# Attention: ACT copies the turned q and k whole out of PSUM, and Pool subtracts their first parts

## The chip, the cores and the metric

The kernel runs on one core of a Trainium2 chip. The metric is the device time of one execution in microseconds (us). The engines of the core are TensorE (PE; its weight loads are shown as PEld), VectorE (DVE), ScalarE (ACT), GpSimd (Pool) and SyncE (SP), which issues transfers.

## The reference

The program is a mixture-of-experts feed-forward layer, then causal attention, then the same feed-forward layer again, on x of 8 x 1024 tokens and 256 channels. The change touches only the attention:

```
q, k, v = (heads(Wq, bq), heads(Wk, bk), heads(Wv, bv))      # 16 heads of 16 dims, y = x W^T + b
q = _apply_rope(q, cos, sin)
k = _apply_rope(k, cos, sin)
att = jnp.einsum('bhqd,bhkd->bhqk', q, k) * (1.0 / np.sqrt(D))
att = jnp.where(causal[None, None], att, NEG_BIG)
att = jax.nn.softmax(att, axis=-1)
y = jnp.einsum('bhqk,bhkd->bhqd', att, v)
```

## The kernel before

The tokens are 64 tiles of 128. A pair of tiles n (32 pairs) is *prepared*: DVE normalises it (L1505), PE transposes it, multiplies with the weights, DVE adds the biases (L1518 for q and k, L1524 for v), Pool rotates q and k (L1402, L1405, L1410, function rope), and PE turns each tile s of the pair back into the bank prep_ps (L1769, transpose_qk). The attention multiplies q and k in bf16, so each 32-bit number is split into three bf16 parts. For tile s this goes round three engines: ACT copies prep_ps to part[0] as bf16 (first_parts, L1665), DVE writes rest = prep_ps - part[0] (leave, L1532), ACT copies rest to part[1] as bf16 (second_parts, L1670), and Pool writes part[2] = rest - part[1] (third_parts, L1414). SP stores the parts to DRAM (L1294) and the v rows (L1297); they are loaded again by group.

A *group* g is four heads of one batch, 32 groups in all. Group g walks through 12 steps t of one half of the queries by one tile of keys. In each step PE makes four scores (L1797, with L1800 for the causal mask) into three banks that take turns, ACT makes the exponentials from them (L1683), and PE multiplies with v (L1810, times_v). For the group after it, PE makes the products for the maxima of the rows (L1786, ring) into three other banks; DVE takes the maxima (L1559 with the mask, L1562 without) and gives the bank back. DVE also splits the maxima into parts (L1576 to L1583), PE turns them (L1779), and Pool issues their transfer (L1426).

The order on each engine is written out by hand. The first five pairs are prepared in a row (the head); then group g finishes pair g+5 (parameter finish) and prepares pair g+6 (prepare). Before the change, in group g: ACT does first_parts(0) after the exponentials of step 1; second_parts(0) and first_parts(1) after those of step 3; second_parts(1) after step 5; and copies the output o (L1675) after step 4. DVE does leave(0) in step 2 and leave(1) in step 4, each after the maxima of its share; in steps 2 and 3 it also measures pair n+1: L1482, L1487, then L1491 and L1492, L1496, L1499 on 128x2 numbers. Pool does the rotation of tile 1 at t = 0 and 1, third_parts at t = 3 and 5, and adds the output bias to x at t = 4 (add_output_bias, L1420); Pool does not wait for the steps, only for its inputs, and takes its list in order. In the head, Pool's list for a pair is: the rotations of both tiles, L1420, then third_parts(0) and (1); DVE does leave(0) and leave(1) after the biases; ACT does first_parts(0), second_parts(0), first_parts(1), second_parts(1), and then the next pair's copy L1660.

PE's transposes of tile 1 and the next pair's transposes (L1730) use the same bank prep_ps, so they wait until leave has read it (rest_ready).

Of the kernel before, what the change touches and what calls it, by code (L numbers as in the profile page):

```python
# [18 lines left out]
ALU = mybir.AluOpType  # L19
# [3 lines left out]
P = 128  # L23
# [1121 lines left out]
def attention_block(nc, sh, dr):  # L1145
# [6 lines left out]
    with ExitStack() as ctx:  # L1152
# [6 lines left out]
        def sem(n):  # L1159
            return ctx.enter_context(nc.semaphore(f"at_{n}"))  # L1160
# [29 lines left out]
        part = [parts[:, a] for a in range(PARTS)]  # L1190
        rest = [sb(f"rest{k}", [P, 2 * CC, P], F32) for k in range(2)]
# [13 lines left out]
        prep_ps = ps("prep_ps", [P, 2 * C])  # L1205
# [17 lines left out]
        rope_step = sem("rope_step")  # L1223
        rot_ready = sem("rot_ready")
        rt_ps_ready = sem("rt_ps_ready")
        part0_ready = sem("part0_ready")
        rest_ready = sem("rest_ready")
        part1_ready = sem("part1_ready")
        part2_ready = sem("part2_ready")
# [147 lines left out]
        def _(pool):  # L1377
# [9 lines left out]
            def rope(n, s, stage):  # L1387
# [20 lines left out]
                if stage == 2:  # L1408
                    pool.wait_ge(rope_step, at + 2)
                    p.tensor_tensor(rot[s][:], by_cos[:], by_sin[:], ALU.add).then_inc(rot_ready, 1)  # L1410

            def third_parts(n, s):
                pool.wait_ge(part1_ready, 2 * n + s + 1)
                p.tensor_tensor(part[2][:, :, s * P:(s + 1) * P], rest[s][:], part[1][:, :, s * P:(s + 1) * P],  # L1414
                                ALU.subtract).then_inc(part2_ready, 1)
# [15 lines left out]
            for n in range(LEAD - 1):  # L1431
                invert_std(n + 1)
                for s in range(2):
                    for stage in range(3):
                        rope(n, s, stage)
                add_output_bias(n)
                for s in range(2):
                    third_parts(n, s)
            invert_std(LEAD)
            for stage in range(3):  # L1440
# [6 lines left out]
            def body(g, k, more, prepare, finish):  # L1447
                n = g + LEAD
                for t in range(NS):
                    if finish:  # L1450
                        if t <= 1:
                            rope(n - 1, 1, t + 1)
                        if t in (3, 5):
                            third_parts(n - 1, t // 4)
                    if prepare and t == 4:
                        add_output_bias(n)
                    if t == 6 and more:
                        move_peaks(g + 1, slot_round(g, k, 1)[0], 0)
                    if prepare:
                        if 5 <= t <= 7 and n + 1 < PAIRS:  # L1460
                            invert_std(n + 1, [t - 5])
                        if 8 <= t <= 10:
                            rope(n, 0, t - 8)
                        if t == 11:
                            rope(n, 1, 0)
                if more:
                    move_peaks(g + 1, slot_round(g, k, 1)[0], 1)
# [4 lines left out]
        def _(dve):  # L1472
# [53 lines left out]
                                           bias[:, 2 * C:3 * C].rearrange("p (g h d) -> p g h d", d=D, h=GH), ALU.add)  # L1526
                last.then_inc(v_ready, 1)

            def leave(n, s):
                dve.wait_ge(part0_ready, 2 * n + s + 1)  # L1530
                dve.wait_ge(part2_ready, 2 * n)
                v.tensor_tensor(rest[s][:], prep_ps[:].rearrange("p (c t) -> p c t", t=P),  # L1532
                                part[0][:, :, s * P:(s + 1) * P], ALU.subtract).then_inc(rest_ready, 1)

            def ring(g, k, r):

                after_last = isinstance(g, int) and g == GROUPS
# [66 lines left out]

            for n in range(LEAD - 1):
                head(n)
                for s in range(2):
                    leave(n, s)
            head(LEAD - 1)
            for r in range(NR):  # L1610
                if RING[r] == SECOND:
# [7 lines left out]
            def body(g, k, more, prepare, finish):  # L1619
                n = g + LEAD  # L1620
                for t in range(NS):
                    if t == 8 and g >= NG and g % NG == 2:
                        dve.wait_ge(sums_loaded, 16 * (g // NG))
                        v.reciprocal(sums[:], sums[:]).then_inc(sums_inverted, 1)
                    for c in range(SHARES):
                        ahead = ring_group(g, t)
                        if ahead is not None:
                            for r in share(t, c):
                                if has_place(ahead, r):
                                    ring(ahead, (k + (2 if t == NS - 1 else 1)) % SLOTS, r)  # L1630
                        if finish:
                            if (t, c) == (2, 0):
                                leave(n - 1, 0)
                            if (t, c) == (4, 1):
                                leave(n - 1, 1)
                        if prepare:
                            if (t, c) == (1, 2):
                                normalize(n)
                            stage = SHARES * (t - 2) + c - 1
                            if 0 <= stage < 6 and n + 1 < PAIRS:  # L1640
                                measure(n + 1, [stage])
                            if (t, c) == (5, 3):
                                xt_low(n)
                            if (t, c) == (7, 1):
                                add_bias_qk(n, 0)
                            if (t, c) == (8, 3):
                                add_bias_v(n)
                            if (t, c) == (11, 1):
                                add_bias_qk(n, 1)
# [4 lines left out]
        def _(act):  # L1654
# [7 lines left out]
            def first_parts(n, s):  # L1662
                act.wait_ge(rt_ps_ready, 2 * n + s + 1)
                act.wait_ge(stored, 16 * PAIR_STORES * n)
                a.copy(part[0][:, :, s * P:(s + 1) * P], prep_ps[:].rearrange("p (c t) -> p c t", t=P)  # L1665
                       ).then_inc(part0_ready, 1)

            def second_parts(n, s):
                act.wait_ge(rest_ready, 2 * n + s + 1)
# [52 lines left out]
        def _(pe):  # L1722
# [38 lines left out]
            def transpose_qk(n, s, half):  # L1761
                if half == 0:
                    pe.wait_ge(rot_ready, 2 * n + s + 1)
                    if s == 0:
                        pe.wait_ge(qk_ready, 2 * n + 2)
                    else:
                        pe.wait_ge(rest_ready, 2 * n + 1)
                for c in range(CC * half, CC * (half + 1)):
                    last = te.transpose(prep_ps[:, c * P:(c + 1) * P], rot[s][:, c * P:(c + 1) * P], sh.ident[:])  # L1769
                if half == 1:  # L1770
                    last.then_inc(rt_ps_ready, 1)
# [44 lines left out]
            pe.wait_ge(ones_ready, 1)  # L1816

            def head(n):
                pe.wait_ge(rest_ready, 2 * n)
                transpose_x(n)  # L1820
                for i in range(3):
                    product_qk(n, 0, i)
                for s in range(2):
                    product_v(n, s)
                for i in range(3):
                    product_qk(n, 1, i)
# [23 lines left out]
            def body(g, k, more, prepare, finish):  # L1850
                n = g + LEAD
                for t in range(NS):
# [11 lines left out]
                    def piece(c):  # L1864
# [5 lines left out]
                        if not prepare:  # L1870
                            return
                        if (t, c) == (5, 0):
                            pe.wait_ge(rest_ready, 2 * n)
                            transpose_x(n)
                        for i in range(3):
                            if (t, c) == (6, i + 1):
# [121 lines left out]
```

## Time and profile before

| | |
|---|---|
| time, median of 3 runs (lowest, highest) | 2623.69 us (2612.97, 2627.59) |
| the profiled execution, time and span | 2642.3 us, 2640.5 us |
| PE busy | 2226.4 us (84%) |
| DVE busy | 1690.9 us (64%) |
| ACT busy | 1249.4 us (47%) |
| Pool busy | 942.5 us (36%) |
| mean granted clock of PE | 0.922 |

Busy time is the time in which an engine works on an instruction; waits are not in it. The attention takes about 600 to 2000 us of the span. Matmuls are pipelined, so PE's busy time is more than the time in which it takes in columns. In the rows, "idle before" is the idle time of the engine in front of an instruction, and "<-" names what ended it.

### The profile page before, as it was taken

How to read it: one execution, taken by the hardware profiler on the slowest of the kernel's cores; microseconds unless marked ns; L12 is line 12 of the kernel's file. 1: busy time of each engine (PE TensorE's matmuls, PEld its weight loads, DVE VectorE, ACT ScalarE, POOL GpSimd, SP SyncE). 2: the span in 40 equal slices, each digit the busy share in tenths (PEclk: the TensorE clock that was granted, in tenths of full speed). 3: DMA queues.
4: the chain of work that ended last, by engine and by line, in shares of the span. 5: the costliest groups of instructions: out<-in, count | busy, mean ns of one | idle time of the engine just before them, and what ended most of it. 6: DMA issues, size and time to landing. Idle time of an engine off the chain costs nothing. (4 is left out here: it accounts for less than half of the span.)

```text
span 2640.5 us, 43228 instructions
## 1 busy us (share of the span) xinstructions
PE 2226.4 (84%) x14740; PEld 1457.2 (55%) x14740; DVE 1690.9 (64%) x5140; ACT 1249.4 (47%) x2506; POOL 942.5 (36%) x1344
## 2 busy tenths in 40 slices
PE   5739999945599999999999999998994773899997
PEld 5729999943334444443444444443332673799997
DVE  7326556533378778788887877887772662465563
ACT  1224444421046656666666665666673432344443
POOL 3534344316523333333333333332000465244442
PEclk9999999975579999999999999999997875999999
DMA  9372322221624453544534435335324423422220
GB/s 347 147 245 69 109 80 72 72 75 40 155 57 100 102 118 81 122 101 99 118 90 114 109 80 114 98 89 118 83 55 125 161 93 126 167 73 97 92 73 22
DMA packets 187148, 283.22 MB, mean 107 GB/s; under 512 B 14616, under 2 KB 149976, under 8 KB 178736
## 3 DMA queue, kind: packets, MB, share of 16 engines
q1 hardware_dynamic: 172592, 247.08, 34.2%
q0 software_dynamic: 14336, 33.38, 3.6%
q8 instruction: 117, 1.92, 0.3%
q14 instruction: 103, 0.84, 0.1%
HBM read 153.99 MB, written 126.88 MB: 106 GB/s over the span
## 5 line engine op out<-in xcount | busy, mean ns | idle before, releaser
L1683 ACT ACTIVATE at_probs<-at_score_ps 128x512 f32<-128x512 f32 (+3 forms) x1536 | 692.5, 497 | 451.3 <-PE at_score_ps L1800 312.0
L1559 DVE CUSTOM_DVE_ANT_0 at_junk<-at_max_ps,at_causal 128x128 f32<-128x128 f32 (+3 forms) x1024 | 485.3, 484 | 124.8 <-PE at_max_ps L1786 123.2
L1786 PE MATMUL at_max_ps<-at_k,at_q 96*128 96x512 bf16 (+3 forms) x1536 | 493.1, 339 | 44.1 <-DVE at_peak L1559 32.0
L1797 PE MATMUL at_score_ps<-at_q,at_k 99*128 99x512 bf16 (+3 forms) x1536 | 498.0, 331 | 9.2 <-DMA at_v<-v_rows 4.2
L1562 DVE TENSOR_REDUCE at_peak<-at_max_ps 128x1 f32<-128x512 f32 x512 | 351.9, 687 | 114.4 <-PE at_max_ps L1786 111.5
L1786 PEld LDWEIGHTS at_max_ps<-at_k,at_q 96*128 96x128 bf16 x1536 | 144.3, 98 | 398.7 <-DVE at_peak L1559 193.6
L1056 DVE TENSOR_TENSOR f_hid_lo<-f_hid,f_hid_hi 128x512 fp32r<-128x512 f32 x256 | 177.4, 693 | 285.2 <-ACT f_hid_hi L1080 274.6
L1810 PE MATMUL at_o_ps<-at_probs,at_v 128*32 128x512 f32 (+3 forms) x3072 | 336.8, 511 | 1.2 <-ACT at_probs L1683 0.7
L1077 ACT ACTIVATE f_hid<-f_hid_ps 128x512 f32<-128x512 f32 x256 | 153.1, 598 | 377.4 <-PE f_hid_ps L1103 374.1
L1118 PE MATMUL f_y_ps<-f_w_hi,f_hid_hi 128*128 128x256 f32 x1024 | 290.7, 284 | 18.5 <-DVE f_hid_lo L1056 18.5
L1118 PE MATMUL f_y_ps<-f_w_hi,f_hid_lo 128*128 128x256 f32 x1024 | 291.1, 284 | 0.0
L1118 PE MATMUL f_y_ps<-f_w_lo,f_hid_hi 128*128 128x256 f32 x1024 | 290.1, 283 | 0.0
L979 POOL TENSOR_SCALAR f_xn<-f_xe 128x256 f32<-128x256 f32 x120 | 164.1, 1374 | 183.1 <-PE f_xt_ps L1091 134.1
L1402 POOL TENSOR_TENSOR at_by_cos<-at_qk,at_cos 128x512 f32<-128x512 f32 x64 | 70.2, 1098 | 436.7 <-DVE at_qk L1518 436.7
L1800 PE MATMUL at_score_ps<-at_hide_bf,ident_bf 128*128 128x128 bf16 x1024 | 225.4, 222 | 0.0
L1797 PEld LDWEIGHTS at_score_ps<-at_q,at_k 99*128 99x128 bf16 x1536 | 150.5, 98 | 123.6 <-ACT at_probs L1683 74.0
L1118 PEld LDWEIGHTS f_y_ps<-f_w_hi,f_hid_hi 128*128 128x128 f32 x1024 | 194.3, 190 | 30.5 <-DVE f_hid_lo L1056 19.4
L1118 PEld LDWEIGHTS f_y_ps<-f_w_lo,f_hid_hi 128*128 128x128 f32 x1024 | 194.0, 189 | 10.4
L1118 PEld LDWEIGHTS f_y_ps<-f_w_hi,f_hid_lo 128*128 128x128 f32 x1024 | 194.0, 189 | 0.0
L1103 PE MATMUL f_hid_ps<-f_xt_hi,f_w_hi 128*128 128x512 f32 x512 | 168.2, 410 | 2.8 <-DVE f_xt_lo L1025 2.8
L1080 ACT CAST f_hid_hi<-f_hid 128x512 fp32r<-128x512 f32 x256 | 159.0, 621 | 8.2
L1103 PE MATMUL f_hid_ps<-f_xt_lo,f_w_hi 128*128 128x512 f32 x512 | 162.3, 398 | 0.0
(178 smaller groups left out, 3647.8 us busy)
## 6 DMA issues: line engine op xcount, KB each, us to landing
f_w_raw<-in_w SPq DMA_DIRECT2D x32, 1024.0 KB, 7.7
qk<-at_parts SPq DMA_DIRECT2D x32, 768.0 KB, 4.2
expert_in<-r_zeros SPq DMA_DIRECT2D x16, 1040.0 KB, 15.9
f_xe<-expert_in SPq DMA_DIRECT2D x32, 520.0 KB, 4.0
v_rows<-at_v_outs SPq DMA_DIRECT2D x32, 512.0 KB, 6.2
at_v<-v_rows SPq DMA_DIRECT2D x32, 512.0 KB, 10.6
o_rows<-at_o_out SPq DMA_DIRECT2D x64, 256.0 KB, 2.0
at_q<-qk SPq DMA_DIRECT2D x32, 384.0 KB, 7.7
```

Of the source, the lines that this page charges most:

```text
L979: last = nc.gpsimd.tensor_scalar(xn[:, t, :], x[:, t, 0:C], x[:, t, MEAN:MEAN + 1], x[:, t, RSTD:RSTD + 1], ALU.subtract, ALU.mult)
L1056: v.tensor_tensor(hid_lo[f % NHID][:], hid[f % NHID][:], hid_hi[f % NHID][:].bitcast(F32), ALU.subtract).then_inc(hid_lo_ready, 1)
L1080: nc.scalar.copy(hid_hi[f % NHID][:], hid[f % NHID][:]).then_inc(hid_hi_ready, 1)
L1103: last = nc.tensor.matmul(hid_ps[f % 2][:], w[ws][:, cc, f * P:(f + 1) * P], x[b % 2][:, cc, :], start=(i == 0), stop=(i == 3 * CC - 1))
L1118: last = nc.tensor.matmul(y_ps[b % 2][t // 2][:, t % 2, :], a[m][:, rows], w[ws][:, f, :], start=(f == 0 and i == 0 and t % 2 == 0), stop= ...
L1559: v.tensor_tensor_reduce(junk[bank(k, r)][:, 0:w], src, causal[:, HALF - w:HALF], 1.0, LEAST, ALU.add, ALU.max, out).then_inc(max_used, 1)
L1562: v.tensor_reduce(out, src, AX.X, ALU.max).then_inc(max_used, 1)
L1683: a.activation(probs[t % 2][:, h, c0:c0 + w], score_ps[(GH * t + h) % BANKS][:, 0:w], ACT.Exp, scale=float(SCALE)).then_inc(exp_done, 1)
L1786: te.matmul(max_ps[bank(u, r)][:, 0:w], q[u][0:ROWS, h, i * P:(i + 1) * P], kk[u][0:ROWS, h, k0:k0 + w], start=True, stop=True).then_inc(m ...
L1797: last = te.matmul(out[:, 0:w], kk[u][:, h, j * P:(j + 1) * P], q[u][:, h, hf * HALF + c0:hf * HALF + c0 + w], start=True, stop=not diagonal)
L1800: last = te.matmul(out[:, 0:P], sh.ident_bf[:], hide_bf[:], start=False, stop=True)
L1810: last = te.matmul(o_ps[h * VW:(h + 1) * VW, c0:c0 + w], vv[u][:, j, h, :], probs[t % 2][:, h, c0:c0 + w], start=(t == FIRST_STEP[hf]), st ...
```

## The change

ACT's first_parts makes a second copy of the bank, whole and in 32 bits, into rest[s], and signals it with a new semaphore, whole_ready; the second copy waits until the third parts of the pair before are made (part2_ready), as leave did. The subtraction rest = rest - part[0] moves from DVE to Pool and now has two SBUF operands. On Pool, leave(0) stands at t = 2 and leave(1) at t = 4 ahead of add_output_bias; in the head both stand after add_output_bias and ahead of the two third_parts. PE's waits for the bank prep_ps are now for whole_ready, so for ACT's second copy. The semaphore part0_ready is gone.

```
+            def leave(n, s):                       # Pool
+                pool.wait_ge(whole_ready, 2 * n + s + 1)
+                p.tensor_tensor(rest[s][:], rest[s][:], part[0][:, :, s * P:(s + 1) * P], ALU.subtract
+                                ).then_inc(rest_ready, 1)
...
                 add_output_bias(n)                  # Pool, head
                 for s in range(2):
+                    leave(n, s)
+                for s in range(2):
                     third_parts(n, s)
...
+                        if t in (2, 4):             # Pool, groups
+                            leave(n - 1, t // 4)
                         if t in (3, 5):
                             third_parts(n - 1, t // 4)
...
-            def leave(n, s):                       # DVE
-                dve.wait_ge(part0_ready, 2 * n + s + 1)
-                dve.wait_ge(part2_ready, 2 * n)
-                v.tensor_tensor(rest[s][:], prep_ps[:].rearrange("p (c t) -> p c t", t=P),
-                                part[0][:, :, s * P:(s + 1) * P], ALU.subtract).then_inc(rest_ready, 1)
...
-                            if (t, c) == (2, 0):
-                                leave(n - 1, 0)
-                            if (t, c) == (4, 1):
-                                leave(n - 1, 1)
...
             def first_parts(n, s):                  # ACT
                 act.wait_ge(rt_ps_ready, 2 * n + s + 1)
                 act.wait_ge(stored, 16 * PAIR_STORES * n)
-                a.copy(part[0][:, :, s * P:(s + 1) * P], prep_ps[:].rearrange("p (c t) -> p c t", t=P)
-                       ).then_inc(part0_ready, 1)
+                turned = prep_ps[:].rearrange("p (c t) -> p c t", t=P)
+                a.copy(part[0][:, :, s * P:(s + 1) * P], turned)
+                act.wait_ge(part2_ready, 2 * n)
+                a.copy(rest[s][:], turned).then_inc(whole_ready, 1)
...
-                        pe.wait_ge(rest_ready, 2 * n + 1)      # PE: transpose_qk; head and step 5 alike
+                        pe.wait_ge(whole_ready, 2 * n + 1)
```

## Rows read from the trace of the kernel before

**Rows 1.** Waits, 900 to 2000 us: total, times, longest in us
```profile
PEld at_max_ps L1786 <- DVE at_peak L1559: 162.5, 249, 1.2
...
PEld at_score_ps L1797 <- ACT at_probs L1683: 64.0, 155, 0.8
```

**Rows 2.** Stretches: length; PE, PEld, DVE, ACT, Pool busy (instructions), PE clock, DMA share, GB/s
```profile
1203.40:1211.80 8.40, 7.23 (x61) 3.16 (x58) 8.33 (x28) 7.42 (x19) 4.32 (x5) 1.00 0.01 2
1212.00:1215.00 3.00, 3.00 (x15) 0.85 (x16) 2.12 (x8) 0.28 (x1) 0.00 (x0) 0.50 0.28 102
1253.00:1256.00 3.00, 2.77 (x23) 1.15 (x23) 3.00 (x11) 1.99 (x8) 0.00 (x0) 1.00 0.23 87
```

**Rows 3.** Timeline of PE, from 1206 us: start, duration, what, idle before
```profile
1211.92 0.61 PE L1786 MATMUL at_max_ps<-at_k,at_q 96*128 96x512 bf16 x1 [0.75 <-DVE at_peak L1559]
```

**Rows 4.** Timeline of DVE, 1203 to 1214 us
```profile
1204.78 1.10 DVE L1505 TENSOR_SCALAR at_xn<-x_sb,at_moments,at_rstd 128x256 f32<-128x256 f32 x2
...
1206.28 0.68 DVE L1532 TENSOR_TENSOR at_rest<-at_prep_ps,at_parts 128x512 f32<-128x512 f32 x1
1206.88 0.67 DVE L1559 CUSTOM_DVE_ANT_0 at_junk<-at_max_ps,at_causal 128x512 f32<-128x512 f32 x1
...
1209.02 1.19 DVE L1491 TENSOR_SCALAR at_half<-at_moments 128x2 f32<-128x2 f32 x1
...
1211.16 0.69 DVE L1559 CUSTOM_DVE_ANT_0 at_junk<-at_max_ps,at_causal 128x512 f32<-128x512 f32 x1
...
1213.35 0.68 DVE L1532 TENSOR_TENSOR at_rest<-at_prep_ps,at_parts 128x512 f32<-128x512 f32 x1
```

**Rows 5.** Three DVE lines, 830 to 1780 us: ns min/median/max, first and last start
```profile
L1491 DVE TENSOR_SCALAR at_half<-at_moments x23: 169/1203/1215, 840.6 to 1741.9; 128x2 f32<-128x2 f32 x23
...
L1496 DVE TENSOR_SCALAR at_bits<-at_bits x23: 156/157/624, 841.3 to 1743.7; 128x2 int32<-128x2 int32 x23
...
L1505 DVE TENSOR_SCALAR at_xn<-x_sb,at_moments,at_rstd x48: 400/535/780, 836.3 to 1778.7; 128x256 f32<-128x256 f32 x48
```

**Rows 6.** Timeline of Pool, 1203 to 1213 us
```profile
1204.14 1.28 POOL L1410 TENSOR_TENSOR at_rot<-at_by_cos,at_by_sin 128x512 f32<-128x512 f32 x1
1207.81 1.16 POOL L1414 TENSOR_TENSOR at_parts<-at_rest,at_parts 128x512 bf16<-128x512 f32 x1 [2.40 <-ACT at_parts L1670]
1208.93 1.26 POOL L1420 TENSOR_TENSOR x_sb<-x_sb,at_bp 128x512 f32<-128x512 f32 x1
```

**Rows 7.** Groups, 900 to 2000 us: busy us, mean ns | idle before, releasers
```profile
L1414 POOL TENSOR_TENSOR at_parts<-at_rest,at_parts 128x512 bf16<-128x512 f32 x46 | 53.2, 1157 | 167.0 <-ACT at_parts L1670 167.0
...
L1675 ACT COPY at_o_out<-at_o_ps 128x512 f32<-128x512 f32 x56 | 33.7, 602 | 0.0
```

**Rows 8.** Timeline of ACT, 1203 to 1213 us
```profile
1203.94 2.54 ACT L1683 ACTIVATE at_probs<-at_score_ps 128x256 f32<-128x256 f32 x7
...
1208.48 2.07 ACT L1683 ACTIVATE at_probs<-at_score_ps 128x512 f32<-128x512 f32 x4
```

**Rows 9.** Timeline of all engines in the head, from 650 and from 715 us
```profile
654.71 1.27 POOL L1420 TENSOR_TENSOR x_sb<-x_sb,at_bp 128x512 f32<-128x512 f32 x1
...
655.96 0.58 ACT L1665 CAST at_parts<-at_prep_ps 128x512 bf16<-128x512 f32 x1 [1.73 <-PE at_prep_ps L1769]
...
658.00 1.16 POOL L1414 TENSOR_TENSOR at_parts<-at_rest,at_parts 128x512 bf16<-128x512 f32 x1 [0.91 <-ACT at_parts L1670]
658.06 1.09 PE L1730 MATMUL at_prep_ps<-ident,at_xn 128*128 128x128 f32 x4 [2.14 <-DVE at_xn L1505]
...
659.18 0.58 ACT L1660 CAST at_xt_hi<-at_prep_ps 128x512 fp32r<-128x512 f32 x1 [1.26 <-PE at_prep_ps L1730]
...
716.14 0.76 DVE L1524 TENSOR_TENSOR at_v_outs<-at_prep_ps,at_bias 128x256 f32<-128x256 f32 x2 [10.53 <-DMA v_rows<-at_v_outs]
```

**Rows 10.** Timeline of DVE in the next two groups: L1491
```profile
1250.74 1.21 DVE L1491 TENSOR_SCALAR at_half<-at_moments 128x2 f32<-128x2 f32 x1
...
1291.07 1.21 DVE L1491 TENSOR_SCALAR at_half<-at_moments 128x2 f32<-128x2 f32 x1
```

More of the change, by code:

```diff
@@ L1225, in attention_block @@
         rt_ps_ready = sem("rt_ps_ready")
-        part0_ready = sem("part0_ready")
+        whole_ready = sem("whole_ready")
         rest_ready = sem("rest_ready")
@@ L1606, in _ @@
                 head(n)
-                for s in range(2):
-                    leave(n, s)
             head(LEAD - 1)
@@ L1630, in body @@
                                     ring(ahead, (k + (2 if t == NS - 1 else 1)) % SLOTS, r)
-                        if finish:
-                            if (t, c) == (2, 0):
-                                leave(n - 1, 0)
-                            if (t, c) == (4, 1):
-                                leave(n - 1, 1)
                         if prepare:
@@ L1818, in head @@
             def head(n):
-                pe.wait_ge(rest_ready, 2 * n)
+                pe.wait_ge(whole_ready, 2 * n)
                 transpose_x(n)
@@ L1872, in piece @@
                         if (t, c) == (5, 0):
-                            pe.wait_ge(rest_ready, 2 * n)
+                            pe.wait_ge(whole_ready, 2 * n)
                             transpose_x(n)
```

## The prediction

> **What bounds the kernel now.** I read the page first for the shares of the engines, then the waits and the groups of the attention stage, then a full timeline of one group, engine by engine, and last the opening of the stage. The change touches only the attention stage: five pairs of tiles prepared one after the other (the head), then 32 groups, of which the first 25 or so also prepare a later pair. In this steady part TensorE (PE) has the longest busy time, but it is not simply the bound: its weight loads wait 162.5 us in 1,100 us for VectorE (DVE) to hand back a bank of maxima, and 64.0 us for ScalarE (ACT) to hand back a bank of scores [rows 1]. So I asked which of the two waits ends last in the steps that the change touches. In the group that starts near 1200 us, DVE is busy 8.33 of 8.40 us from 1203.4 to 1211.8, ACT 7.42, Pool 4.32 [rows 2]. At the end of it PE sits idle 0.75 us for DVE's L1559 before its next maxima, at 1211.92 [rows 3]. Walking back from there, DVE's own order fills the stretch: the normalisation L1505 (1.10 us for two), the subtraction L1532 at 1206.28, statistics, L1491 with 1.19 us, and L1559 at 1211.16 [rows 4]. That is the chain to change. The second L1532 of the group falls at 1213.35 [rows 4], after PE has been released, so it is off this chain.
>
> **The oddest row** is L1491. It works on 128x2 numbers, and costs 169 ns at least, 1,203 in the median of 23 groups [rows 5]. In the group shown it starts at 1209.02, just after Pool's L1420 started at 1208.93, and ends at 1210.21, just after L1420's end at 1210.19 [rows 4, 6]. L1496 is 157 ns in the median and 624 at most, L1505 400 to 780 [rows 5]; the one of 780 in this group started at 1204.78 and so ended 0.14 us after Pool's L1410 (1204.14 + 1.28). So in this kernel a DVE instruction that takes one SBUF tile and writes SBUF stands still while a Pool elementwise operation runs, if Pool came first. The Trainium skill, page "SBUF — State Buffer", section "Who interferes with whom", says the same of such a pair: the two share a port pair, held for a whole instruction, and the later one blocks fully. This trace agrees, with 169 against 1,203 ns. What this means for the change is below.
>
> **Part 1, DVE loses 64 subtractions** of 0.68 us [rows 4], 43.5 us of busy time in all; back to back they overlap, and the first of a group takes 0.60 us of the chain (1206.28 to the next start, 1206.88) [rows 4]. With 25 groups that is 15 us at most for the first ones. The second ones lie beside PE's work; if they were on the chain too, another 15 us.
>
> **Part 2, ACT gains 64 whole copies.** Nearest rows: L1675, a copy of the same 128x512 from PSUM to a 32-bit tile, 602 ns [rows 7], and L1665, the same to bf16, 0.58 us [rows 9]. I take 0.58 each. In a group the first comes ahead of the seven exponentials at 1203.94, which run without a gap for 2.54 us; the second ahead of the four at 1208.48 [rows 8]. ACT is full there, so PE's score banks come 0.58 us later after the first and about 1.1 us later after the second. Cover: PE is ahead of DVE in the maxima, which is why DVE has no gap in the stretch. Without the cover the full 1.1 us a group would show. PE's transposes of the second tile will wait for ACT's copy, done at about 1204.6, and not for DVE's subtraction, done at 1206.96; nothing is gained by it while the scores beside them are late.
>
> **Part 3, Pool gains 64 subtractions.** Nearest rows: L1414, the same 32-bit minus bf16 operands, 1,157 ns [rows 7], and L1410, all 32-bit, 1.28 us [rows 6]; I take 1.16. The results of Pool are not late for anyone: Pool can have the first done at 1204.14 + 1.28 + 1.16 = 1206.6, and ACT's L1670, which takes some 0.6 us and releases L1414 at 1207.81, starts after that. But queued behind it on Pool stand L1414 and L1420. L1414 waits for ACT's L1670, which moves by ACT's 0.58 us to about 1208.3, so it runs 1208.35 to 1209.5. The second subtraction, whose input ACT has by about 1209.55, runs to 1210.75, and L1420 to 1212.0. Where Pool was busy 1207.81 to 1210.19, it is now busy without a gap from 1208.35 to 1212.0, and in this time DVE wants to run L1491, L1492, L1496 and L1499, each of the kind of rows 5.
>
> **How this meets DVE.** With 0.6 us taken off, DVE reaches L1491 at 1208.4, within 0.1 us of the start of Pool's L1414. If Pool is first, L1491 ends at 1209.5; the next L1559 takes 0.65; L1496 at 1210.15 falls into the moved subtraction and ends at 1210.8; L1499 waits for its result and comes right behind, by when L1420 has started (Pool's operations follow each other without a gap, 1207.81 + 1.16 and 1208.93), and ends with it at 1212.03. The L1559 that started at 1211.16 starts at 1212.0: PE is released 0.85 us later than now. The second L1505 may be blocked too, by the moved first subtraction: it would lose between nothing and 1.0 us, by who gets the port between two Pool operations, which these rows do not show. By the page's rule that the order of issue decides, it would lose the whole 1.0. It matters little: DVE then comes to L1491 at 1209.4 instead of 1208.4, still inside L1414, and the end of the Pool run at 1212.0 sets the rest in both cases. If instead DVE is first with L1491 and L1492, only L1496 waits inside L1414 and L1499 inside the subtraction, to 1210.65; then PE's products, late by ACT's 1.1 us, are the bound. My estimate: exponentials from 1209.55 on, the first done by 1210.15 (2.07 us for four, rows 8, and the engine's delay), a score and the product for the maxima behind it some 0.6 us, DVE 0.7 us on it (L1559, rows 4), so that PE is released at about 1211.6, 0.3 us earlier than now.
> I take the first, since three of the four ways to arrive (Pool first at L1491, the second L1505 blocked, PE's maxima late) lead to it: +0.85 us x 25 groups = +21 us.
>
> **Part 4, the head.** Here nothing overlaps much, and the order of Pool's queue decides. Now: ACT L1665 at 655.96, PE's transposes of the next pair 658.06, ACT L1660 659.18 [rows 9]. After: the first subtraction stands on Pool behind the rotation and L1420 (654.71 + 1.27), so it runs 655.95 to 657.1; ACT, which does L1670 of the first tile before L1665 of the second, starts L1665 at 657.7 and the whole copy at 658.2, done 658.8; PE transposes 658.85 to 659.95. Pool's second subtraction runs 658.85 to 660.05, ACT's L1670 to 660.65, and only then comes L1660 in ACT's order: 660.65 against 659.18, +1.5 us for each of the four steps from one pair to the next, +6. Pool's third parts end at 660.05 + 1.16 + 1.16 = 662.35 instead of 659.16 (658.00 + 1.16), so the stores of a pair start 3.2 us later. The sixth pair waits for such a store (L1524, idle 10.53 us) [rows 9], which itself stands behind the loads of the first groups: its landing moves by 3 x 1.5 + 3.2 = 7.7 to 4 x 1.5 + 3.2 = 9.2. I take +8.5 us for the head. A bound below: if only PE's 0.8 us a pair counted, +4.
>
> **Part 5, TensorE's clock.** From 1212 to 1215 the granted clock is 0.50, so the lower level of 1.2 GHz; in the same place of the next group, 1253 to 1256, it is 1.00 [rows 2]. PE had sat idle for 0.75 us just before the first [rows 3]. L1491 starts at 1209.02, 1250.74 and 1291.07: the group with the low clock takes 41.72 us, the other 40.33 [rows 4, 10], so a fall costs 1.4 us. Over 22 intervals from 840.6 to 1741.9 [rows 5] the mean is 40.97, so about half of the groups have it. A longer idle time of PE in front of this place could bring it into all (+1.4 x 13 = +18), a shorter one could remove it (-1.4 x 12 = -17). I take no change.
>
> **Sum.** +21 + 8.5 = +29.5, on the profiled execution's 2642.3 us 2671.8. That execution is 18.6 us above the median of the runs, 2623.69; I put the same difference on the median: 2653.
>
> **The rivals.**
> A (0.55): the forecast, Pool's unbroken run holds up DVE. 2653, and from 2640 to 2680 with the clock's term.
> B (0.24): DVE slips in ahead of Pool, and ACT's copies cap the gain at 0.3 us a group: -8 + 8.5 = about 0, 2624, within 12 either way by the clock. For it: the margin at L1491 is 0.1 us. Against it: L1491 is blocked now in most groups.
> C (0.16): DVE is the chain and is simply relieved: 0.6 us x 25 = 15 saved, up to 23 if some of the second subtractions count, and the low clock goes from half of the groups (-17), against +8.5 in the head: -6.5 to -31, about 2603. It decides if PE's maxima stay at least 0.6 us ahead of DVE in spite of ACT, and if L1491, L1496 and L1499 together wait no more than the 1.03 us (1.203 - 0.169) of now. For it: DVE's 8.33 of 8.40. Against it: ACT's 7.42 of 8.40 and both of its copies ahead of full runs.
> D (0.05): ACT's 1.1 us shows fully as well, beside the blocked DVE: 2685 or more.
>
> The change surely does what it says: the operations are moved, so "no effect" is only B's balance.
>
> **Numbers.** The measurement tells about 0.5% (13 us) from no change. Slower: A and D, 0.60. Within: B's middle and the upper edge of C, 0.23. Faster: the rest of C and a corner of B, 0.17. The range holds A with its clock, B, and the upper part of C: 2612 to 2680. The likeliest case alone is 2640 to 2680.
>
> **What would show it.** In the profile after: ACT's whole copy near 0.58 us x64; Pool's moved subtraction 1.16 to 1.28 us; L1491, L1496 and L1499 together longer than now (0.169 to 1.2 each), and L1505's median above 535 ns; PE's release in this place later; in the head, the first L1660 after a subtraction 1.5 us later per pair. Wrong I am if the DVE instructions after the subtraction stay as they are: then B or C holds, and groups with L1491's spacing below 40.3 us would show it.

## The result, and the profile after

The changed kernel takes 2644.69 us in the median (2640.40 to 2646.77, four runs), against 2623.31 us (2612.97 to 2627.59, four runs) for the kernel before on the same chip. The ratio is 1.0084 with a 95% interval of 1.0063 to 1.0104: 21 us slower. The forecast of 2653 was 8 us too high. The sign is right, and 2644.69 lies in the range, also in the narrower one of the likeliest case.

First the page's busy times, then the groups of the stretch 900 to 2000 us (busy us, mean ns | idle before, releaser). The lines moved: L1500, L1505, L1508 and L1514 are what L1491, L1496, L1499 and L1505 were; L1414 is now Pool's moved subtraction, L1419 its third parts, L1425 the output bias; L1662 is ACT's first part, L1664 its whole copy.

```profile
PE 2209.5 (84%) x14740; PEld 1456.3 (55%) x14740; DVE 1699.4 (64%) x5076; ACT 1278.3 (48%) x2570; POOL 1016.6 (38%) x1408
```

```profile
L1414 POOL TENSOR_TENSOR at_rest<-at_rest,at_parts 128x512 f32<-128x512 f32 x46 | 54.3, 1181 | 2.4 <-ACT at_rest L1664 2.2
...
L1514 DVE TENSOR_SCALAR at_xn<-x_sb,at_moments,at_rstd 128x256 f32<-128x256 f32 x44 | 42.6, 1008 | 0.0
...
L1664 ACT COPY at_rest<-at_prep_ps 128x512 f32<-128x512 f32 x46 | 27.5, 597 | 0.0
L1508 DVE TENSOR_SCALAR at_rstd<-at_bits 128x2 int32<-128x2 int32 x21 | 23.8, 1135 | 0.7
L1505 DVE TENSOR_SCALAR at_bits<-at_bits 128x2 int32<-128x2 int32 x21 | 11.6, 551 | 0.0
L1500 DVE TENSOR_SCALAR at_half<-at_moments 128x2 f32<-128x2 f32 x21 | 5.7, 269 | 0.7
```

The oddest thing is in the first line. DVE lost 64 subtractions of 0.68 us, 43.5 us of work, and is busy 8.5 us *longer* than before (1699.4 against 1690.9). The time is in lines with small operands, here by their means in the groups. L1508, on 128x2 numbers, takes 1,135 ns where it took 170; L1505 takes 551 where it took 179. The normalisation L1514, of which each group has two, takes 1,008 where it took 584, so 0.85 us more a group. Only L1500 went the other way, from 1,154 to 269. I call it "the port" when DVE stands still behind a Pool operation in this way: it is lost in other places than before, and for longer.

The same place of a group as rows 3, 4 and 6 show, in the timeline (start, duration, what, idle before):

```profile
1206.45 1.16 POOL L1419 TENSOR_TENSOR at_parts<-at_rest,at_parts 128x512 bf16<-128x512 f32 x1 [1.73 <-ACT at_parts L1668]
...
1207.42 0.22 DVE L1500 TENSOR_SCALAR at_half<-at_moments 128x2 f32<-128x2 f32 x1
1207.43 2.09 ACT L1681 ACTIVATE at_probs<-at_score_ps 128x512 f32<-128x512 f32 x4
...
1207.63 1.16 POOL L1414 TENSOR_TENSOR at_rest<-at_rest,at_parts 128x512 f32<-128x512 f32 x1
...
1208.11 0.39 PE L1795 MATMUL at_score_ps<-at_q,at_k 99*128 99x512 bf16 x1 [0.45 <-ACT at_probs L1681]
...
1208.23 0.58 DVE L1505 TENSOR_SCALAR at_bits<-at_bits 128x2 int32<-128x2 int32 x1
...
1208.75 1.26 POOL L1425 TENSOR_TENSOR x_sb<-x_sb,at_bp 128x512 f32<-128x512 f32 x1
1208.85 1.19 DVE L1508 TENSOR_SCALAR at_rstd<-at_bits 128x2 int32<-128x2 int32 x1
...
1209.95 0.68 DVE L1562 CUSTOM_DVE_ANT_0 at_junk<-at_max_ps,at_causal 128x512 f32<-128x512 f32 x1
...
1210.69 0.39 PE L1784 MATMUL at_max_ps<-at_k,at_q 96*128 96x512 bf16 x1 [1.26 <-DVE at_peak L1562]
```

Pool runs L1419, L1414 and L1425 from 1206.45 to 1210.01 without a gap, 3.56 us; the forecast had 3.65. In it DVE's L1505 starts at 1208.23 inside L1414 and ends at 1208.81, when L1414 ends (1208.79); L1508 starts behind it at 1208.85, by when L1425 has begun, and ends at 1210.04, when L1425 ends (1210.01). L1562 follows, and PE gets its bank, after 1.26 us of idle time. DVE has no idle time on the way there: it is busy 8.33 of the 8.40 us from 1201.6 to 1210.0, as it was in the same place before [rows 2]. But L1500 at 1207.42 slips in between L1419 (ends 1207.61) and L1414 (starts 1207.63), and takes 0.22 us.

The waits of PE's matmuls, not of its weight loads as in rows 1, from 850 to 1750 us (total, times, longest):

```profile
PE at_max_ps L1784 <- DVE at_peak L1562: 25.8, 23, 1.3
PE at_score_ps L1795 <- ACT at_probs L1681: 19.4, 44, 0.6
```

In the same stretch of before PE waits 26.6 us for the maxima, and for ACT's exponentials not at all. The second row is new: 44 times, twice a group, 0.44 us each, just where the two whole copies stand.

The clock, by stretches as in rows 2 (the PE clock is the third figure from the end, ahead of DMA share and GB/s):

```profile
1207.40:1210.70 3.30, 1.59 (x13) 0.47 (x9) 3.25 (x9) 2.95 (x8) 2.59 (x3) 1.00 0.00 0
1211.00:1214.00 3.00, 3.00 (x29) 1.51 (x28) 2.66 (x14) 1.67 (x5) 0.63 (x1) 1.00 0.28 100
```

The stretch that had 0.50 before [rows 2] has 1.00 now, though the last piece of idle time ahead of it is longer. Between 800 and 1800 us, some 24 groups, the granted clock fell to 0.50 ten times for 3.41 us before, and twice after.

**How the groups are measured from here on.** A group's period is the spacing of its first small DVE line (at_half), from the source row: (last start - first start) / (count - 1). Before it is 40.97 [rows 5]. Because falls of the clock come and go, I also give the *full-clock period*, the median spacing of the first exponentials of neighbouring groups over the groups with no fall. It is 40.31 us before and 40.75 after, +0.44.

```profile
L1500 DVE TENSOR_SCALAR at_half<-at_moments x23: 210/222/1044, 838.6 to 1739.7; 128x2 f32<-128x2 f32 x23
```

Here the period is (1739.7 - 838.6) / 22 = 40.96, so in this stretch of the profiled executions the two kernels' groups are equally long: +0.44 at full clock, less the falls that are gone.

**The head.** The next two fences are source rows and the timeline of after:

```profile
L1656 ACT CAST at_xt_hi<-at_prep_ps x6: 578/578/586, 584.1 to 694.9; 128x512 fp32r<-128x512 f32 x6
```

```profile
644.76 1.27 POOL L1425 TENSOR_TENSOR x_sb<-x_sb,at_bp 128x512 f32<-128x512 f32 x1
645.99 1.15 POOL L1414 TENSOR_TENSOR at_rest<-at_rest,at_parts 128x512 f32<-128x512 f32 x1
...
648.17 0.59 ACT L1664 COPY at_rest<-at_prep_ps 128x512 f32<-128x512 f32 x1
...
648.84 1.16 POOL L1414 TENSOR_TENSOR at_rest<-at_rest,at_parts 128x512 f32<-128x512 f32 x1 [1.70 <-ACT at_rest L1664]
...
650.03 0.62 ACT L1668 CAST at_parts<-at_rest 128x512 bf16<-128x512 f32 x1 [1.27 <-POOL at_rest L1414]
650.55 0.58 ACT L1656 CAST at_xt_hi<-at_prep_ps 128x512 fp32r<-128x512 f32 x1
```

The spacing of the pairs is (694.9 - 584.1) / 5 = 22.16 us, against 20.70 before (five starts of L1660, 597.1 to 679.9): +1.46, forecast +1.5. The fence shows the forecast's own chain: the first subtraction behind L1425, the second behind the second whole copy, ACT's L1668 behind that, and only then L1656. From the first L1656 to the first exponential it is 160.89 us, against 152.21: +8.7, forecast +8.5. Counted from the same start, the sixth pair's biases, which wait for the store (L1524 before), begin at 127.06 us against 119.05, +8.0, where the forecast had 7.7 to 9.2.

### The profile page after: what moved, and what is told of

It reads as the page before. It is cut to its first block and busy times, and to the rows that moved or that the text cites. A ratio compares the mean times of both kernels' runs of the same rounds, so it can differ in the third digit from the quotient of the medians.

```text
span 2645.0 us, 43228 instructions
## 1 busy us (share of the span) xinstructions
PE 2209.5 (84%) x14740; PEld 1456.3 (55%) x14740; DVE 1699.4 (64%) x5076; ACT 1278.3 (48%) x2570; POOL 1016.6 (38%) x1408
## 5 line engine op out<-in xcount | busy, mean ns | idle before, releaser
L1562 DVE CUSTOM_DVE_ANT_0 at_junk<-at_max_ps,at_causal 128x128 f32<-128x128 f32 (+3 forms) x1024 | 483.3, 484 | 132.5 <-PE at_max_ps L1784 130.1
L1808 PE MATMUL at_o_ps<-at_probs,at_v 128*32 128x512 f32 (+3 forms) x3072 | 330.5, 502 | 1.2 <-ACT at_probs L1681 0.7
```

Source lines behind the costliest of these rows:

```text
L1562: v.tensor_tensor_reduce(junk[bank(k, r)][:, 0:w], src, causal[:, HALF - w:HALF], 1.0, LEAST, ALU.add, ALU.max, out).then_inc(max_used, 1)
L1808: last = te.matmul(o_ps[h * VW:(h + 1) * VW, c0:c0 + w], vv[u][:, j, h, :], probs[t % 2][:, h, c0:c0 + w], start=(t == FIRST_STEP[hf]), st ...
```

## The experiments

Where a kernel leaves part of the computation out, its paragraph says so. Every kernel was timed beside the kernel before, whose medians were 2622.82, 2625.19 and 2624.27 us in the three sets.

| kernel | median us | ratio, 95% interval | period | full-clock period |
|---|---|---|---|---|
| before | 2623 to 2625 | 1 | 40.97 | 40.31 |
| after | 2644.69 | 1.0084, 1.0063 to 1.0104 | 40.96 | 40.75 |
| head_on_dve | 2633.04 | 1.0037, 1.0022 to 1.0052 | 40.95 | 40.75 |
| head_order | 2635.47 | 1.0047, 1.0031 to 1.0062 | 41.09 | 40.77 |
| pool_alone | 2652.26 | 1.0115, 1.0099 to 1.0132 | 41.87 | 41.39 |
| act_alone | 2611.19 | 0.9962, 0.9948 to 0.9976 | 40.29 | 40.04 |
| no_subtract | 2592.42 | 0.9883, 0.9866 to 0.9900 | 39.57 | 39.40 |
| before_bias_late | 2592.73 | 0.9886, 0.9867 to 0.9905 | 39.42 | 39.30 |
| after_bias_late | 2618.52 | 0.9975, 0.9958 to 0.9993 | 40.10 | 39.83 |
| head_bias_late | 2606.59 | 0.9943, 0.9921 to 0.9966 | 40.03 | 39.83 |
| act_bias_late | 2609.44 | 0.9942, 0.9920 to 0.9964 | 39.97 | 39.89 |
| after_both_late | 2612.82 | 0.9957, 0.9940 to 0.9974 | 39.99 | 39.80 |
| before_both_late | 2589.98 | 0.9871, 0.9846 to 0.9895 | 39.64 | 39.26 |
| no_subtract_bias_late | 2583.66 | 0.9842, 0.9816 to 0.9867 | 39.15 | 38.91 |

### The head: head_on_dve and head_order

head_on_dve is after, but in the head (n < LEAD - 1) the subtraction is DVE's again and ACT makes no whole copy; the groups are as after.

```
+                if n < LEAD - 1:                      # ACT, first_parts
+                    a.copy(part[0][:, :, s * P:(s + 1) * P], turned).then_inc(part0_ready, 1)
+                    return
...
                 head(n)                               # DVE
+                for s in range(2):
+                    leave(n, s)
```

> The changed kernel, but in the head (the first five pairs) the first parts are subtracted by VectorE as before; the groups are as changed. If the head costs what its profile shows (from the first copy to xt_hi to the first exponential 152.2 us before, 160.9 after), this is 8.7 us faster than the changed kernel, so about 2636, 12 us above the kernel before. If the groups cost nothing and the head is the whole loss, it is level with the kernel before, 2623. In its profile the groups should keep the changed kernel's 40.93 us each.

Measured: 2633.04, 11.7 us below after and 9.7 above before. Its period is after's, and from the first exponential to the last it takes 1256.9 us (after 1255.8, before 1250.2).

head_order is after with another order in the head's Pool list alone:

```
+                leave(n, 0)
                 add_output_bias(n)
-                for s in range(2):
-                    leave(n, s)
+                leave(n, 1)
```

> The changed kernel; only in the head Pool does the first tile's subtraction ahead of the output bias (L1425) and the second's behind it. If the place in Pool's queue makes the head's loss: 1.2 us less per pair, the first copies to xt_hi 21.0 apart instead of 22.16 (20.7 before), 5 to 7 us less than the changed kernel, 2638. If the longer way round (ScalarE, Pool, ScalarE instead of ScalarE, VectorE, ScalarE) makes it: no change.

Measured: 2635.47, 9 us below after. Pairs follow each other by 20.95 us in the middle of the head (after 22.16), and from the first xt_hi to the first exponential it takes 153.1 us instead of 160.9. So most of the head's cost was not the work moved but its place behind the output bias; this order takes some 9 of the 12 us back.

### One part alone: pool_alone, act_alone, no_subtract

pool_alone is before, and Pool makes an extra subtraction of the same size at the places of the moved ones (in place on its tile rot, after PE has turned it, so nothing uses the result; DVE keeps its subtraction).

```
+            def extra(n, s):
+                pool.wait_ge(part0_ready, 2 * n + s + 1)
+                p.tensor_tensor(rot..., rot..., part[0][:, :, s * P:(s + 1) * P], ALU.subtract)
...
+                        if t in (2, 4):
+                            extra(n - 1, t // 4)
```

> The kernel before plus only Pool's two extra subtractions per group (t = 2 and 4), on data that nobody reads afterwards; VectorE and ScalarE do all they did. Port theory: VectorE's L1505, L1496 and L1499 wait behind Pool's longer run, 0.5 to 1.0 us a group lost, +13 to +25 us, less what the clock gives back (its falls may vanish, up to -17). Theory that ScalarE's copies and the head make the loss: Pool is idle enough, no change, 2623 within 5, and the three lines keep their durations.

act_alone is before, and in the groups ACT makes a whole copy into rest ahead of its first part; DVE overwrites it.

```
+                if n >= LEAD - 1:
+                    act.wait_ge(part2_ready, 2 * n)
+                    a.copy(rest[s][:], turned)
+                a.copy(part[0][:, :, s * P:(s + 1) * P], turned).then_inc(part0_ready, 1)
```

> The kernel before plus only ScalarE's whole copy per tile in the groups (VectorE overwrites its result with the subtraction as before). Port theory: ScalarE's 1.2 us a group lie beside VectorE's chain, +0 to +5 us. ScalarE theory: PE's waits for score banks grow and show, 0.4 to 1.1 us a group, +11 to +30 us.

no_subtract is before without DVE's subtraction in the groups; it leaves that part of the computation out.

```
-                                leave(n - 1, 0)
...
-                                leave(n - 1, 1)
```

> The kernel before with the subtraction left out in the groups (rest keeps what the head left in it; nobody else does it, and the bank is released by ScalarE's first copy). It shows what VectorE's relief is worth without its price. If VectorE is the chain: 0.6 us a group, -16 us, and up to -17 more if PE's clock no longer falls: 2590 to 2608. If something else takes over at once (L1491 just waits as long behind Pool's L1420, whose time is set by ScalarE): within 5 of 2623.

Groups of the three kernels, 900 to 1750 us, in this order:

```profile
L1511 DVE TENSOR_SCALAR at_xn<-x_sb,at_moments,at_rstd 128x256 f32<-128x256 f32 x42 | 40.9, 1014 | 0.0
...
L1497 DVE TENSOR_SCALAR at_half<-at_moments 128x2 f32<-128x2 f32 x21 | 19.5, 930 | 0.7
...
L1502 DVE TENSOR_SCALAR at_bits<-at_bits 128x2 int32<-128x2 int32 x20 | 12.6, 631 | 0.0
```

```profile
L1496 DVE TENSOR_SCALAR at_bits<-at_bits 128x2 int32<-128x2 int32 x21 | 13.2, 627 | 0.0
...
L1491 DVE TENSOR_SCALAR at_half<-at_moments 128x2 f32<-128x2 f32 x21 | 9.8, 467 | 0.7
```

```profile
L1491 DVE TENSOR_SCALAR at_half<-at_moments 128x2 f32<-128x2 f32 x21 | 12.2, 581 | 0.7
L1496 DVE TENSOR_SCALAR at_bits<-at_bits 128x2 int32<-128x2 int32 x21 | 12.0, 569 | 0.0
```

Pool's extra work alone costs 29 us (+1.08 a group), more than I expected: +0.86 us is in the two normalisations (1,014 ns against 584 each), and the small lines together take 0.28 more. DVE has no idle time between them and PE's release, which comes 1.08 us later. The relief alone gives 30 us (-0.91 a group, and all but one of the falls of the clock go). It is not the relief alone: DVE comes to L1491 0.6 us earlier and so meets Pool's operations at other moments. The miss is act_alone: I expected it to cost nothing or something, and it is 11.6 us *faster* than before. Adding work to ACT made the kernel faster: it delays Pool's inputs (Pool's third parts start 11.48 us after the group's first exponential instead of 10.99), the small lines meet Pool's run elsewhere, and L1491 takes 467 ns in the mean instead of 1,154. So ACT's copies can't be priced while L1420 is in the way. Nor do the three add up: +1.08 - 0.91 - 0.27 is -0.10, and the whole change measures +0.44.

### L1420's collision taken out: before_bias_late and its relatives

Pool's output bias (L1420, 1.27 us) is the last of its run, and no input of it is made in the steps around it. before_bias_late is before with that one call moved from t = 4 to t = 7, into Pool's free time behind the small 128x2 work; after_bias_late, head_bias_late and act_bias_late are after, head_on_dve and act_alone with the same move.

```
-                    if prepare and t == 4:
-                        add_output_bias(n)
...
+                        if t == 7:
+                            add_output_bias(n)
```

> The kernel before with one move: Pool adds the output bias to x (L1420) at t = 7, after its Newton steps, instead of t = 4. Port theory: L1491, which now costs 1,154 ns in the mean because L1420 has just begun, drops to about 0.17, and VectorE's chain loses 1.0 us a group; with the falls of the clock gone as in the run with ScalarE's copies alone, 39.3 to 39.6 us a group, -26 to -40 us. If the port only hides another wait: as before within 5.

> The changed kernel with the same move of L1420 to t = 7. Port theory: its last VectorE wait of the run (L1499's, 1,135 ns) goes, L1505's (1,008) and L1496's (0.55) stay: 0.5 to 1.0 us a group less than the changed kernel, -12 to -27 us, so 2618 to 2632. If ScalarE's copies or something else hold the groups at 40.75, nothing changes: 2645 within 5.

> As the run before this one, and the head on VectorE as in the kernel before: 8 to 12 us less than that run. If the groups come to below 40.0 us, this is level with or faster than the kernel before.

> The kernel before with L1420 at t = 7 and ScalarE's extra whole copy per tile in the groups; VectorE still subtracts. It asks what holds the changed kernel with L1420 at t = 7 at 39.83 us a group, where the kernel before with that move is at 39.30. If ScalarE's copies do: 39.7 to 39.9 here too, 2605 to 2610. If L1505's longer wait behind Pool's first subtraction does (not present here): 39.3, 2593 within 5.

The line of before_bias_late that answers to rows 5, and those of after_bias_late, both from the groups 900 to 1750 us:

```profile
L1491 DVE TENSOR_SCALAR at_half<-at_moments 128x2 f32<-128x2 f32 x21 | 3.6, 170 | 0.7
```

```profile
L1505 DVE TENSOR_SCALAR at_bits<-at_bits 128x2 int32<-128x2 int32 x21 | 12.3, 588 | 0.0
...
L1508 DVE TENSOR_SCALAR at_rstd<-at_bits 128x2 int32<-128x2 int32 x21 | 4.5, 216 | 0.7
```

In before, one moved call takes L1491 from 1,154 ns in the mean to 170, -0.98 us, and the full-clock period falls by 1.01: the wait stood wholly on the chain. All but one of the ten falls of the clock are gone too, and the kernel is 32 us faster. In after it takes L1508 from 1,135 to 216, -0.92, and the period falls by 0.92. This shows in both kernels that a 128x2 line behind the output bias is on the path of the group. head_bias_late, 2606.59, is 12 us below after_bias_late, as head_on_dve was below after.

The waits of PE (850 to 1750 us) for act_bias_late:

```profile
PE at_score_ps L1800 <- ACT at_probs L1686: 20.1, 46, 0.4
...
PE at_max_ps L1789 <- DVE at_peak L1559: 5.6, 23, 0.6
```

With L1420's collision out of the way, ACT's copies cost +0.59 us a group (39.30 to 39.89) and 15 to 17 us in time (2592.73 to 2609.44, and 0.9886 against 0.9942, each beside its own before). PE now waits 46 times for the exponentials, 0.44 us each; before_bias_late has no such row. L1491 is longer here too, 465 ns against 170, but that is not the price: DVE then sits idle for 0.31 us for PE's product ahead of its next L1559, in the median of the groups, where before_bias_late has no idle time. So with the output bias out of the way there is no cover for ACT's copies.

The port is not out of the way in all of these kernels. In after_bias_late Pool's moved subtraction still holds up L1514 (1,010 ns) and L1505 (588), and DVE has no idle time up to PE's release, 14.79 us after the group's first exponential. In act_bias_late, by ACT alone, the release is at 14.69, and in before_bias_late at 14.11. So DVE behind Pool and ACT's copies are two limits side by side, each about 0.6 us later than before, and the later one counts.

### What is left of it: after_both_late, before_both_late, no_subtract_bias_late

The first two also start the normalisation of the next pair (L1514, L1505 before) later, to keep it out of Pool's first subtraction:

```
-                            if (t, c) == (1, 2):
+                            if (t, c) == (2, 1):
                                 normalize(n)
```

> The changed kernel with L1420 at t = 7 and the normalisation (two L1505s) moved from (t, c) = (1, 2) to (2, 1), where Pool should be idle. Its mean should fall from 1,010 to about 400 ns. If that wait holds the groups: 39.3 or less, 13 us or more less than with the first move alone, about 2605. If ScalarE's copies hold them: 39.8 as before the move, 2618.

> The kernel before with both moves. Mean of L1505 from 586 to about 400 ns. Port theory with VectorE as the chain: 0.2 to 0.4 us a group less than with the first move alone (39.30), -5 to -10 us, 2583 to 2588. If the chain is elsewhere by now: 2593.

```profile
L1514 DVE TENSOR_SCALAR at_xn<-x_sb,at_moments,at_rstd 128x256 f32<-128x256 f32 x44 | 16.1, 408 | 0.0
```

The row is after_both_late's, in the same view: 408 ns instead of 1,010, and the period moves only from 39.83 to 39.80. Without that wait DVE sits idle instead, 0.73 us for PE's product, and then waits for the end of Pool's subtraction at L1505 (605 ns) all the same: PE's release stays at 14.79. So in this kernel the large wait costs nothing. Its time, 2612.82, is some 5 us better than after_bias_late's, about what the two intervals allow; before_both_late, 2589.98, can't be told from before_bias_late, where I had expected a few us.

no_subtract_bias_late is no_subtract with the late bias (it leaves out the groups' subtraction).

```
-                                leave(n - 1, 0)
...
+                        if t == 7:
+                            add_output_bias(n)
```

> The kernel before with L1420 at t = 7 and without the subtraction in the groups (left out). The most that any move of the subtraction away from VectorE could give once the port is free: 38.4 to 38.8 us a group and 2567 to 2580, if VectorE is the chain there; 39.3 and 2593 if it is not.

Measured: 2583.66, less of a gain than I expected. It is 9 us below before_bias_late, -0.39 us a group, and ACT's copies alone cost more: 0.59. But it is not the most that the relief can give, as I had taken it to be, for the port is not free in it: DVE comes to L1491 0.6 us earlier, into Pool's third parts, and L1491 takes 576 ns instead of 170.

## Why the prediction was right, and where not

**What bounds the kernel** was read rightly: DVE's maxima release PE in the touched steps, and L1491 is the row to look at. That L1491's wait is real time on the path, all of it, is now shown by before_bias_late.

**Part 1, the relief,** forecast 0.60 us on the chain, measures 0.91 (no_subtract) with the output bias at t = 4 and 0.39 with it late. So it is no fixed number, and the 0.52 between the two is about what the port makes of it: in the first pair of kernels L1491 and L1496 together get shorter by 0.18 (1,333 to 1,150 ns), in the second longer by 0.40 (334 to 734). Without either, the relief is 0.7 to 0.8 us a group, an estimate from these rows: the forecast 0.60 and a little of the second subtraction.

**Part 2, ACT's cost.** Its size was right (597 ns forecast as 580). ACT is late as forecast, if less: the first exponential of step 4 is 12.46 us after the group's first, against 11.66, +0.8 where the forecast had about 1.1. PE's wait for ACT appears in every kernel with the copies (0.44 us, twice a group) and in none without. "Cover: PE is ahead of DVE in the maxima, which is why DVE has no gap in the stretch" held in the changed kernel: DVE has no idle time there up to the release. But it holds only because DVE stands behind Pool for so long. With L1420 moved, the price of the copies shows: 0.59 us a group.

**Part 3, Pool.** Duration 1,181 ns against 1,160 forecast; the run without a gap is as forecast, and L1496 and L1499 are blocked in turn, as forecast. L1491 is not: "DVE reaches L1491 at 1208.4, within 0.1 us of the start of Pool's L1414" was to leave it blocked for 1.1 us. In the trace it comes up before the end of the third parts (L1419, the old L1414), waits for it, and gets through ahead of the moved subtraction. The forecast left open who gets the port between two Pool operations. After shows it: a DVE instruction that was waiting got in between two of them, here in 222 ns in the median of 23. The Trainium skill, page "SBUF — State Buffer", section "Who interferes with whom", says that the order of issue decides who blocks. L1500 agrees, as far as the trace tells: it starts at 1207.42, L1414 at 1207.63. The second normalisation is blocked, as the page's rule would have it (it ends 0.85 us later). The forecast said that this matters little, since the end of Pool's run sets the rest; the trace fits that, and after_both_late shows it for the kernel with the output bias late, but no run shows it for the changed kernel as it stands. The prediction's sentence on which DVE instructions stand still is too wide. In before, 50 of 50 L1487 (128x2 from 128x6, both in SBUF) started while a long Pool operation ran and took 157 ns in the mean, and L1482 took 404 beside Pool and 416 without it. The page ties the block to DVE's two-port modes, which it says tensor_scalar, the kind of L1491, L1496, L1499 and L1505, can enter.

**The groups' term: +21 us, mis-sized.** "The L1559 that started at 1211.16 starts at 1212.0: PE is released 0.85 us later than now" became 0.60 us: from the group's first exponential to the start of the multiplication with v of step 4 it is 16.16 us instead of 15.56. A part of it is made up in the rest of the group, and the full-clock period grows by 0.44 us. Over 25 groups that is +11 us. The forecast let the whole delay stand in the group's length. All of the 0.60 can be followed on DVE, which has no idle time in either kernel: -0.60 for the subtraction and +0.85 for the second normalisation bring it to L1500 0.25 us later (12.45 us after the first exponential instead of 12.20), and from there to the release it takes 0.35 more. The end is fixed by Pool: its run begins at 11.48, 0.49 later than before because ACT's L1668 is late (forecast 0.54), and lasts 3.56 us (forecast 3.65); L1508 ends with it at 15.06, and the release comes 0.68 behind its end. So the likeliest case, "Pool's unbroken run holds up DVE", was right on what holds the changed kernel here, and the size of the term was wrong.

It does not follow that the port alone makes the loss. With the output bias late in both kernels, after still loses as much (39.30 to 39.83, +0.53). There two limits lie side by side, DVE behind Pool's subtraction (release at 14.79) and ACT (14.69), so that taking away one of them would leave the other. They can't be added up, and no run has Pool's subtraction alone with the output bias late.

**Part 4, the head: right.** +8.7 measured in the trace for +8.5, by the chain that was forecast: +1.46 a pair, and +8.0 at the biases that wait for the store. head_on_dve puts it at 11.7 us in time, whose uncertainty takes in both.

**Part 5, the clock.** "I take no change" was wrong in the profiled execution: ten falls became two, at 1.4 us each some 11 us that hide the 11 us of the period. It was to be worse with a longer idle time. In the sum the idle time hardly changed (PE waits 26.6 us for the maxima before and 25.8 after), but it comes in one piece of 1.26 us instead of two of 0.55 and 0.75 (the last is in [rows 3]), and the clock stayed. What in PE's activity decides it, these runs don't settle. Nor do they settle whether the unprofiled executions have as many falls.

**The sum.** Head +8.7, first to last exponential +5.6, together 14 of the 21 us in the two profiled executions. Of the 5.6, 3.7 lie in groups 25 and 26 and 1.7 in the first two; between them the falls of the clock that are gone hide what the groups lose. By the medians, head_on_dve splits it as 11.7 (head) and 9.7 (groups), where the forecast had 8.5 and 21. So the groups' term was about twice too large and the head came out somewhat above its own; that the forecast time is off by only 8 us is in part luck. That the medians' 9.7 is 4 us more than the trace's 5.6 is within the intervals (0.0022 to 0.0052 of 2623 is 6 to 14 us). The profiled execution of before was 18.6 us above its median, and 13 of these lie before the attention: it starts at 573.6 us there, at 560.3 in after's, and between 559 and 561.5 in the other twelve kernels' too. So a comparison of spans (2640.5, 2645.0) would have shown almost nothing.

**The rivals.** B (DVE slips in ahead) happened for one line of three, L1500, and did not decide the release. Its other half, that ACT's copies cap the gain, is what act_bias_late shows once the output bias is late. C (simple relief) fails with it: L1500, L1505 and L1508 together take longer than their lines before, and ACT's copies cost more than the 0.39 of the relief. Version to keep: the kernel before with the one moved call, 2592.73 us, 1.1% faster than before. The change with the same move is 0.9% above it (0.9975 against 0.9886).

## What to carry to other kernels

When work is to move to Pool, first look for small SBUF-to-SBUF instructions of DVE whose duration is many times their minimum: a 128x2 line of 1.2 us was as long as the Pool instruction beside it. What counts is which Pool instructions run back to back near such a line, so the cheapest repair is often to move a Pool instruction that nobody waits for, and only then to ask about moving work. A copy "hidden" behind another engine's wait must be priced again once that wait is gone: here it cost 0.59 us a group, after it had looked like a gain. And where two limits lie side by side, the prices of single edits don't add up.

## What was not expected of the hardware

A DVE instruction that was already waiting got the port between two Pool instructions that follow each other without a gap: L1500 ended at 1207.64, L1414 started at 1207.63 after L1419's end at 1207.61, and 222 ns is its median over 23 groups, against 169 to 170 undisturbed and 1,203 when it starts just behind a Pool instruction. DVE's lines with a PSUM operand did not lengthen: L1532 has a mean of 680 ns in before_bias_late and 680 in act_alone, and the five of before that started while a long Pool operation ran took 692 ns, no more than the longest of the others. And the granted clock fell ten times in some 24 groups with 0.75 us of idle time last ahead of the place, but twice with 1.26 us. Where PE waits less for the maxima in total (10.6 us in before_bias_late against 26.6) there is one fall.
